# TensorE's products that nobody reads left out of the heads and tails of all stages other than the attentions

## The chip, the cores and the metric

The kernel runs on one core of a Trainium2 chip. The metric is the device time of one launch in microseconds (us). TensorE (PE in the profile) multiplies matrices, and its weight loads have rows of their own (PEld); VectorE is DVE, ScalarE is ACT, GpSimd is POOL, and SP issues the transfers. The profile gives TensorE's granted clock as a share of its full speed: 1.00 is 2.4 GHz and 0.50 is 1.2 GHz.

## The reference

The input x is (4, 256, 256), 1024 tokens of 256 channels, and so is a context `ctx`. Four decoder layers follow each other, each with a self-attention, a cross-attention to the context and a feed-forward part, each on a layer-normed x and added to x:

```python
x = x + _L0_attn_ref(_layernorm(x, axis=-1), ...)      # capped scores
x = x + _L0_xattn_ref(_layernorm(x, axis=-1), ctx_2048, ctx_2048)
x = x + _L0_ffn_ref(...)                               # fp4 weights, gelu
x = x + _L1_attn_ref(...)                              # token and channel mixing, no attention
x = x + _L1_xattn_ref(...)
x = x + _L1_ffn_ref(...)                               # eight experts of different widths, top 2
x = x + _L2_attn_ref(...)                              # 32 heads of 8
x = x + _L2_xattn_ref(_layernorm(x, axis=-1), ctx_2048)
x = x + _L2_ffn_ref(...)                               # sixteen experts, top 4, and a shared one
x = x + _L3_attn_ref(...)                              # 16 heads of 16
x = x + _L3_xattn_ref(...)                             # a scan over the tokens
x = x + _L3_ffn_ref(...)                               # ternary weights, silu
```

## The kernel before

X holds x in SBUF as eight tiles of 128 tokens (`TT` = 8), and HT the normed x with channels in the partitions. The kernel is a row of stages; each is a block in which every engine has its own list of instructions, in the order of the code, tied to the others by semaphores. All engines meet at the end of a block, and none begins the next before the last has come there; the view of waits names the line of the block then (`PEq L1054` and the like). The stages, with the time of the first TensorE entry: `project` and `capped_attention` (layer 0), `cross_attention` (from 153 us), `mlp` (214.9), `mixing` (280.1), `cross_attention` (361.7), `experts1` (416.9), `project_paired` (531.7) and `shifted_attention` (563.9) of layer 2, `cross16` (703.3), `experts2` (799.7), `project_paired` (1111.2) and `shifted_attention` (1146.3) of layer 3, `wkv_scan` (1227.9), and `ternary_mlp` (1273.9).

Most stages begin with a layer norm, `norm_steps`: for each pair g of token tiles VectorE takes the moments (`measure`), ScalarE the root (`root`), VectorE scales into H (`apply`, L300), TensorE turns four 128x128 blocks (`turn`, L363), and ScalarE copies them into HT (`copy`, L331, or as the first of three bf16 parts, L333 to L337 with L305 and L309 on VectorE). The stage's own products wait for two pairs of it (`columns`).

Between these steps TensorE's list holds calls of `warm`, n products of the bf16 identity with itself, 512 columns each, into a bank of PSUM that nobody reads:

```python
    def warm(pe, bank, n):
        for _ in range(n):
            pe.matmul(PS[:, bank, :].rearrange("p (a n) -> p a n", a=4), identb[:],
                      identb[:].rearrange("p (a n) -> p a n", a=1).to_broadcast([P, 4, P]), start=True, stop=True)
```

They wait for nothing and nothing waits for them by a semaphore, but TensorE takes them in order with the rest. All of them have line L241. The attentions (`shifted_attention`) have such calls too, at their head, in their first steps and at their tail (20 products at the tail of a cross-attention, 4 at that of a self-attention).

Of the kernel before, what the change touches and what calls it, by code (L numbers as in the profile page):

```python
# [131 lines left out]
def build_decoder(nc, x, ctx, wa, wb, wl, w2f, vec, rowv, const, out):  # L132
# [105 lines left out]
# [5 lines that stand above are left out]
# [797 lines left out]
    def project_paired(w, hd, V, spread, arrived=None, **norm_of):  # L1040
# [8 lines left out]
        with ExitStack() as st:  # L1049
# [4 lines left out]
            with nc.Block() as block:  # L1054
                @block.tensor
                def _(pe):
                    if arrived is not None:
                        pe.wait_ge(*arrived)
                    warm(pe, 3, 8)
                    norm["turn"](pe, 0)  # L1060
                    warm(pe, 3, 4)
                    norm["turn"](pe, 1)
                    warm(pe, 3, 3)
                    for n, (a, _, j, c) in enumerate(work):
# [22 lines left out]
                        last.then_inc(S["v_proj"], 1)  # L1087
                    warm(pe, 6, 18)

# [244 lines left out]
    def mlp(n, up, down, bias, **norm_of):  # L1334
# [3 lines left out]
        with ExitStack() as st:  # L1338
# [7 lines left out]
            with nc.Block() as block:  # L1346
                @block.tensor
                def _(pe):
# [20 lines left out]

                    warm(pe, 3, 8)  # L1370
                    for g in range(TT // 2):
                        norm["turn"](pe, g)
                        warm(pe, 3, 4)
                    for c in range(NCH):
# [59 lines left out]
    def mixing():  # L1434
# [7 lines left out]
        with ExitStack() as st:  # L1442
# [20 lines left out]
            bank_out = lambda g: (0, 1, 3, 6)[g]  # L1463
            bank_cv = lambda g: (2, 5, 4, 7)[g]

            with nc.Block() as block:
# [101 lines left out]
                def _(pe):  # L1568
# [97 lines left out]
                    for f in range(sum(FB1)):  # L1666
                        if f % 4 == 0:
                            warm(pe, bank_out(1), 1)
                        last = pe.matmul(PS[:, bank_out(0), 0:1], wB("w2")[:, f * P:(f + 1) * P], gelu_b1[:, f:f + 1],
                                         start=f == 0, stop=f == sum(FB1) - 1)  # L1670
                    last.then_inc(S["bias_sum"], 1)
                    warm(pe, bank_out(1), 16)

# [72 lines left out]
    def experts1():  # L1746
# [9 lines left out]
        with ExitStack() as st:  # L1756
# [17 lines left out]
            with nc.Block() as block:  # L1774
# [10 lines left out]
                def _(pe):  # L1785
# [22 lines left out]

                    warm(pe, 0, 8)
                    for c in range(NCH):  # L1810
                        norm["turn"](pe, 2 * c)
                        warm(pe, 0, 4)
                        norm["turn"](pe, 2 * c + 1)
                        warm(pe, 0, 3)
                        norm["columns"](pe, 2 * c + 1)
                        for k in range(KD):
                            last = pe.matmul(PS[:, 2 + c, :], wB("down", KD)[:, k, :], HT[:, k, c * CH:(c + 1) * CH],
                                             start=k == 0, stop=k == KD - 1)
                        last.then_inc(S["narrow"], 1)
# [10 lines left out]

                    warm(pe, 4, 6)
                    pe.wait_ge(S["gates"], d["gates"] + 1)
# [114 lines left out]
    def experts2(sums, over_partitions, scales, replace):  # L1947
# [7 lines left out]
        with ExitStack() as st:  # L1955
# [15 lines left out]
            with nc.Block() as block:  # L1971
# [27 lines left out]
                def _(pe):  # L1999
# [19 lines left out]

                    warm(pe, 7, 8)  # L2020
                    norm["turn"](pe, 0)
                    warm(pe, 7, 4)
                    norm["turn"](pe, 1)
                    warm(pe, 7, 3)
                    norm["columns"](pe, 1)
# [348 lines left out]
    def ternary_mlp(exact, SC, parts):  # L2374
# [5 lines left out]
        with ExitStack() as st:  # L2380
# [6 lines left out]
            with nc.Block() as block:  # L2387
                @block.tensor
                def _(pe):
# [22 lines left out]

                    warm(pe, 3, 8)
                    for g in range(TT // 2):
                        norm["turn"](pe, g)
                        warm(pe, 3, 4)
                    warm(pe, 3, 6)
                    for c in range(NCH):
# [205 lines left out]
```

## Time and profile before

| what | value |
|---|---|
| time, median of 3 runs | 1354.63 us (1352.7 to 1359.07) |
| the profiled execution, its own time | 1354.48 us |
| its span, first to last instruction | 1352.7 us |
| TensorE busy | 1227.5 us, 91% |
| VectorE, ScalarE, GpSimd busy | 57%, 41%, 25% |
| DMA | 47.24 MB, mean 35 GB/s |

The profile comes from one execution. A busy TensorE includes the products that nobody reads, and says nothing of the clock; the row of granted clock does. In a timeline row the first number is the start, the second the length, and what stands in brackets is the idle time before it and who ended it. A float32 product is recorded as two entries (a turn's blocks as one each), so that "x4" of 128x512 in float32 is two products of the program.

### The profile page before, as it was taken

What the parts mean: (1) busy time and instruction counts of PE and PEld (TensorE: products, weight loads), DVE (VectorE), ACT (ScalarE), POOL (GpSimd) and SP (SyncE); (2) the same over time, 40 slices, a digit from 0 to 9 for tenths busy, and PEclk for the clock granted to TensorE, in tenths of its full rate; (3) what the DMA queues carried; (4) which work ended last, traced back from release to release, by engine and by line L of the source; (5) the groups of instructions that cost most, each with busy time, mean ns of one, the idle gap of its engine ahead of it and who ended that gap; (6) DMA issues with size and microseconds to landing.
All of it is one profiled execution on the core that took longest, in us unless ns stands there. A gap on an engine that the chain in (4) does not pass through costs nothing. (4 is left out here: it accounts for less than half of the span.)

```text
span 1352.7 us, 23648 instructions
## 1 busy us (share of the span) xinstructions
PE 1227.5 (91%) x9359; PEld 739.4 (55%) x9374; DVE 769.2 (57%) x2069; ACT 554.3 (41%) x1096; POOL 334.2 (25%) x376
## 2 busy tenths in 40 slices
PE   5878897969998998999998999999999999996898
PEld 3456543658654444566664545555555555663455
DVE  6733586585785346678866745242111126778955
ACT  4777054643354243644444544111111115446453
POOL 2454012000022000445541312232222223451100
PEclk9988998979999999999999998999999999997899
DMA  9000000000220300000000000223322300000000
GB/s 373 0 2 1 1 2 1 0 1 0 117 88 1 125 0 1 1 3 2 3 2 1 2 1 12 68 66 96 95 82 85 106 17 1 2 2 0 0 1 31
DMA packets 13341, 47.24 MB, mean 35 GB/s; under 512 B 1688, under 2 KB 4888, under 8 KB 12464
## 3 DMA queue, kind: packets, MB, share of 16 engines
q1 hardware_dynamic: 13232, 45.74, 10.0%
q8 instruction: 74, 1.21, 0.4%
q14 instruction: 35, 0.29, 0.1%
HBM read 44.59 MB, written 1.15 MB: 34 GB/s over the span
## 5 line engine op out<-in xcount | busy, mean ns | idle before, releaser
L827 ACT ACTIVATE PT<-PS 128x384 f32<-128x384 f32 (+1 forms) x320 | 153.2, 531 | 185.7 <-PE PS L640 138.3
L2007 PE MATMUL PS<-HT,WA 128*128 128x512 f32 x448 | 201.6, 593 | 2.4 <-DVE MO L2085 2.0
L2085 DVE TENSOR_TENSOR MO<-PS,AO 128x512 f32<-128x512 f32 x56 | 38.7, 691 | 205.9 <-ACT AO L2075 205.8
L2075 ACT ACTIVATE AO<-PS 128x512 f32<-128x512 f32 x56 | 33.3, 597 | 247.9 <-PE PS L2007 247.8
L2007 PEld LDWEIGHTS PS<-HT,WA 128*128 128x128 f32 x448 | 84.6, 190 | 87.7 <-issue 82.9
L760 DVE CUSTOM_DVE_ANT_0 junk<-PS,TRI 128x128 bf16<-128x128 f32 (+1 forms) x384 | 112.6, 353 | 4.0 <-PE PS L621 0.2
L241 PE MATMUL PS<-identb 128*128 128x512 bf16 x420 | 105.2, 390 | 4.9 <-PEq L593 1.8
L2015 PE MATMUL PS<-WA,HO 128*128 128x256 f32 x448 | 105.5, 378 | 0.0
L2015 PEld LDWEIGHTS PS<-WA,HO 128*128 128x128 f32 x448 | 84.5, 189 | 34.7 <-issue 24.9
L2140 POOL TENSOR_TENSOR HO<-MO,GR 128x512 f32<-128x512 f32 x44 | 57.8, 1314 | 168.6 <-PE PS L2015 168.6
L621 PE MATMUL PS<-KS,QM 32*128 32x128 f32 (+1 forms) x768 | 86.7, 347 | 7.5 <-DVE QM L794 6.6
L640 PE MATMUL PS<-QM,KS 32*128 32x256 f32 (+1 forms) x768 | 88.5, 347 | 0.0
L799 DVE RECIPROCAL OD<-OD 128x256 f32<-128x256 f32 x40 | 69.9, 1747 | 31.0 <-ACT OD L835 25.9
L868 POOL TENSOR_SCALAR_AFFINE_SELECT PT<-PT 128x512 f32<-128x512 f32 x96 | 60.8, 634 | 99.1 <-ACT PT L827 99.1
L878 POOL TENSOR_TENSOR OD<-OD 128x256 f32<-128x256 f32 x24 | 17.4, 726 | 270.9 <-DVE OD L799 270.9
L621 PEld LDWEIGHTS PS<-KS,QM 32*128 32x128 f32 x768 | 65.8, 184 | 30.2 <-DVE QM L794 16.6
L709 PE MATMUL PS<-PT,CST 128*32 128x256 f32 (+1 forms) x1280 | 75.3, 353 | 0.0
L241 PEld LDWEIGHTS PS<-identb 128*128 128x128 bf16 x420 | 39.2, 100 | 54.4 <-issue 19.4
L640 PEld LDWEIGHTS PS<-QM,KS 32*128 32x128 f32 x768 | 65.6, 184 | 1.9 <-issue 1.2
L709 PE MATMUL PS<-PT,VM 128*32 128x256 f32 (+1 forms) x1024 | 58.3, 345 | 2.0 <-POOL PT L868 1.8
L1115 POOL TENSOR_TENSOR ROT<-RC,RS 128x512 f32<-128x512 f32 x16 | 20.3, 1270 | 149.0 <-DVE RS L1104 147.7
L1931 DVE SCALAR_TENSOR_TENSOR HB<-HA,ROW,GB 128x512 f32<-128x512 f32 x40 | 30.1, 751 | 40.6 <-ACT HA L1866 36.1
(323 smaller groups left out, 2398.1 us busy)
## 6 DMA issues: line engine op xcount, KB each, us to landing
WA<-w2f_in SPq DMA_DIRECT2D x28, 384.0 KB, 4.3
WA<-wl_in SPq DMA_DIRECT2D x1, 5137.0 KB, 15.3
GR<-gate_rows SPq DMA_DIRECT2D x20, 256.0 KB, 3.8
GB<-gate_rows SPq DMA_DIRECT2D x8, 512.0 KB, 7.0
WB<-wb_in SPq DMA_DIRECT2D x1, 3208.0 KB, 19.2
WA<-wa_in SPq DMA_DIRECT2D x1, 2560.0 KB, 14.7
WA<-wa_in SPq DMA_DIRECT2D x1, 1792.0 KB, 15.5
GR<-gate_rows SPq DMA_DIRECT2D x4, 448.0 KB, 3.9
```

Of the source, the lines that this page charges most:

```text
L241: pe.matmul(PS[:, bank, :].rearrange("p (a n) -> p a n", a=4), identb[:], identb[:].rearrange("p (a n) -> p a n", a=1).to_broadcast([P, 4, ...
L621: return pe.matmul(PS[:, s, m * T:m * T + n], queries(U, v)[rows, m * P:(m + 1) * P], keys(U, v)[rows, 0:n], start=True, stop=True, skip_g ...
L640: last = pe.matmul(bank, keys(U, v)[rows, n * P:(n + 1) * P], queries(U, v)[rows, lo:hi], start=n == 0, stop=r > 1, skip_group_check=True, ...
L709: last = pe.matmul(PS[at:at + 32, 7, what * T + lo:what * T + hi], lhs, src, start=what == 0 and v == 0 and n == 0, stop=v == r - 1 and n ...
L760: last = dve.tensor_tensor_reduce(junk[:, s, m * P:m * T + P], PS[:, s, m * T:m * T + (m + 1) * P], TRI[:, (1 - m) * P:T], 1.0, NEG, ALU.a ...
L799: dve.reciprocal(o, o).then_inc(S["at_inv"], 1)
L827: act.activation(PT[:, g % 3, st_slot(k), 0:W], PS[:, st_bank(g, k), 0:W], ACT.Exp, scale=scale).then_inc(S["at_exp"], 1)
L868: pool.affine_select(v, v, [[0, 4], [1, P]], ALU.is_ge, 0.0, base=0, channel_multiplier=-1).then_inc(S["at_masked"], 1)
L2007: last = pe.matmul(PS[:, 2 * c + half, :], chunk(i, half)[:, k * P:(k + 1) * P], HT[:, k, c * CH:(c + 1) * CH], start=k == 0, stop=k == KD ...
L2015: last = pe.matmul(PS[:, 4 + t // 2, (t % 2) * D:(t % 2 + 1) * D], HO[:, c, j * P:(j + 1) * P], chunk(i, 2), start=i == 0 and t % 2 == 0, ...
L2085: dve.tensor_tensor(MO[:, c], PS[:, 2 * c + 1, :], AO[:, c], ALU.mult).then_inc(S["mult_out"], 1)
L2140: pool.tensor_tensor(HO[:, c], MO[:, c], gate[:, c * CH:(c + 1) * CH], ALU.mult).then_inc(S["pool_mark"], 1)
```

## The change

Each `warm` call outside `shifted_attention` goes. 184 of 420 such products go: 24 in `mlp` (8 at the head, 4 behind each turn), 21 in `mixing` (five singles among the twenty products with one column, L1669, and 16 at the tail), 28 in `experts1` (22 at the head, 6 ahead of the turns of the gates), 15 at the head and 18 at the tail of each of the two `project_paired`, 15 at the head of `experts2`, 30 at the head of `ternary_mlp`. Nothing else differs, so that the other engines have the lists that they had.

```diff
--- before.py
+++ after.py
@@ -1056,11 +1056,8 @@
                 def _(pe):
                     if arrived is not None:
                         pe.wait_ge(*arrived)
-                    warm(pe, 3, 8)
                     norm["turn"](pe, 0)
-                    warm(pe, 3, 4)
                     norm["turn"](pe, 1)
-                    warm(pe, 3, 3)
                     for n, (a, _, j, c) in enumerate(work):
 
                         if n == 0:
@@ -1085,7 +1082,6 @@
                             last = pe.matmul(PS[:, 4 + t % 2, 0:D], HT[:, k, t * P:(t + 1) * P], w["v"][:, k, :],
                                              start=k == 0, stop=k == KD - 1)
                         last.then_inc(S["v_proj"], 1)
-                    warm(pe, 6, 18)
 
                 @block.vector
                 def _(dve):
@@ -1367,10 +1363,8 @@
                                                  skip_group_check=True)
                         last.then_inc(S["down_ps"], 1)
 
-                    warm(pe, 3, 8)
                     for g in range(TT // 2):
                         norm["turn"](pe, g)
-                        warm(pe, 3, 4)
                     for c in range(NCH):
                         go_up(0, c)
                     for i in range(n):
@@ -1664,12 +1658,9 @@
                     pe.wait_ge(S["mx_gate"], 2)
                     pe.wait_ge(S["bias_gelu"], 1)
                     for f in range(sum(FB1)):
-                        if f % 4 == 0:
-                            warm(pe, bank_out(1), 1)
                         last = pe.matmul(PS[:, bank_out(0), 0:1], wB("w2")[:, f * P:(f + 1) * P], gelu_b1[:, f:f + 1],
                                          start=f == 0, stop=f == sum(FB1) - 1)
                     last.then_inc(S["bias_sum"], 1)
-                    warm(pe, bank_out(1), 16)
 
                 @block.scalar
                 def _(act):
@@ -1806,12 +1797,9 @@
                                                  wB("core", KD)[:, k, :], start=k == 0, stop=k == KD - 1)
                         last.then_inc(S["o_proj"], 1)
 
-                    warm(pe, 0, 8)
                     for c in range(NCH):
                         norm["turn"](pe, 2 * c)
-                        warm(pe, 0, 4)
                         norm["turn"](pe, 2 * c + 1)
-                        warm(pe, 0, 3)
                         norm["columns"](pe, 2 * c + 1)
                         for k in range(KD):
                             last = pe.matmul(PS[:, 2 + c, :], wB("down", KD)[:, k, :], HT[:, k, c * CH:(c + 1) * CH],
@@ -1828,7 +1816,6 @@
                     for g in range(TT // 2):
                         core(g)
 
-                    warm(pe, 4, 6)
                     pe.wait_ge(S["gates"], d["gates"] + 1)
                     for t in range(TT):
                         last = pe.transpose(PS[0:E, 4 + t // 4, (t % 4) * P:(t % 4 + 1) * P], G[:, t, :], ident)
@@ -2017,11 +2004,8 @@
                                              skip_group_check=True)
                         last.then_inc(S["down_ps"], 1)
 
-                    warm(pe, 7, 8)
                     norm["turn"](pe, 0)
-                    warm(pe, 7, 4)
                     norm["turn"](pe, 1)
-                    warm(pe, 7, 3)
                     norm["columns"](pe, 1)
                     go_up(0, 0)
                     norm["turn"](pe, 2)
@@ -2410,11 +2394,8 @@
                                                  skip_group_check=True)
                         last.then_inc(S["down_ps"], 1)
 
-                    warm(pe, 3, 8)
                     for g in range(TT // 2):
                         norm["turn"](pe, g)
-                        warm(pe, 3, 4)
-                    warm(pe, 3, 6)
                     for c in range(NCH):
                         go_up(0, c)
                     for i in range(n):
```

The head of layer 2's `project_paired` on TensorE, before (L363 is a turn, L1077 the query and key projection, L1085 the value projection):

```order
L1055 UNCONDITIONAL_BRANCH
L241 MATMUL PS<-identb 128x512 x8
L363 MATMUL PS<-CST,H 128x128 x4
L241 MATMUL PS<-identb 128x512 x4
L363 MATMUL PS<-CST,H 128x128 x4
L241 MATMUL PS<-identb 128x512 x3
L1077 MATMUL PS<-HT,WA 128x512 x2
L1085 MATMUL PS<-WA,HT 128x256 x2
```

and after the change, whose line numbers are smaller by three from there on:

```order
L1055 UNCONDITIONAL_BRANCH
L363 MATMUL PS<-CST,H 128x128 x8
L1074 MATMUL PS<-HT,WA 128x512 x2
L1082 MATMUL PS<-WA,HT 128x256 x2
L363 MATMUL PS<-CST,H 128x128 x4
```

The first two turns stand next to each other and are the only work ahead of the projections.

The tail of the same stage and the head of its attention on TensorE, before (L621 is a product of scores):

```order
L1077 MATMUL PS<-HT,WA 128x512 x2
L1085 MATMUL PS<-WA,HT 128x256 x2
L241 MATMUL PS<-identb 128x512 x18
L1054 UNCONDITIONAL_BRANCH
L599 UNCONDITIONAL_BRANCH
L621 MATMUL PS<-KS,QM 128x256 x2
L621 MATMUL PS<-KS,QM 128x128 x2
L621 MATMUL PS<-KS,QM 128x256 x2
L621 MATMUL PS<-KS,QM 128x128 x2
L241 MATMUL PS<-identb 128x512 x8
```

and after the change:

```order
L1074 MATMUL PS<-HT,WA 128x512 x2
L1082 MATMUL PS<-WA,HT 128x256 x2
L1054 UNCONDITIONAL_BRANCH
L599 UNCONDITIONAL_BRANCH
L621 MATMUL PS<-KS,QM 128x256 x2
L621 MATMUL PS<-KS,QM 128x128 x2
L621 MATMUL PS<-KS,QM 128x256 x2
L621 MATMUL PS<-KS,QM 128x128 x2
L241 MATMUL PS<-identb 128x512 x8
```

Eighteen products go from the end of the block; the attention's own eight stay.

The head of `experts1` on TensorE up to the turns of the gates, before (L1817 narrows to 128 channels, L1822 is the router, L1793 an expert's first product, L1805 the core product, L1834 the turns of the gates):

```order
L363 MATMUL PS<-CST,H 128x128 x4
L241 MATMUL PS<-identb 128x512 x3
L1817 MATMUL PS<-HT,WB 128x512 x2
L363 MATMUL PS<-CST,H 128x128 x4
L241 MATMUL PS<-identb 128x512 x4
L363 MATMUL PS<-CST,H 128x128 x4
L241 MATMUL PS<-identb 128x512 x3
L1817 MATMUL PS<-HT,WB 128x512 x2
L1822 MATMUL PS<-WB,HT 128x8 x16
L1793 MATMUL PS<-GH,WB 128x512 x2
L1805 MATMUL PS<-WB,H 128x256 x16
L241 MATMUL PS<-identb 128x512 x6
```

and after the change:

```order
L363 MATMUL PS<-CST,H 128x128 x8
L1805 MATMUL PS<-HT,WB 128x512 x2
L363 MATMUL PS<-CST,H 128x128 x8
L1805 MATMUL PS<-HT,WB 128x512 x2
L1810 MATMUL PS<-WB,HT 128x8 x16
L1784 MATMUL PS<-GH,WB 128x512 x2
L1796 MATMUL PS<-WB,H 128x256 x16
L1821 MATMUL PS<-CST,G 8x128 x8
```

The last two turns follow each other, and the turns of the gates follow the core product directly.

## Rows read from the trace of the kernel before

**Rows 1.** The page: its first line, and TensorE's granted clock in 40 slices.

```profile
span 1352.7 us, 23648 instructions
PEclk9988998979999999999999998999999999997899
```

**Rows 2.** The view of the cores: span and mean granted clock.

```profile
core 0: 1352.7 us, clock 0.963
```

**Rows 3.** The page's groups: the products that nobody reads (busy us, mean ns).

```profile
L241 PE MATMUL PS<-identb 128*128 128x512 bf16 x420 | 105.2, 390 | 4.9 <-PEq L593 1.8
```

**Rows 4.** Windows, TensorE alone: us, busy (entries), granted clock, DMA share, GB/s.

```profile
223.90:229.10 5.20, 0.05 (x1) 0.73 0.00 0
229.10:233.10 4.00, 3.94 (x10) 0.50 0.00 0
...
432.90:436.20 3.30, 0.00 (x0) 0.74 0.00 0
436.20:441.30 5.10, 5.05 (x8) 0.50 0.00 0
...
1257.10:1260.50 3.40, 3.40 (x5) 0.50 0.00 0
```

**Rows 5.** Timeline, TensorE, the start of `mlp`'s products.

```profile
229.16 5.79 PE L1356 MATMUL PS<-parts,WA 128*128 128x512 bf16 x17 [5.22 <-DVE parts L309]
```

**Rows 6.** Windows of all engines (PE, PEld, DVE, ACT, POOL; then clock, DMA).

```profile
361.70:366.70 5.00, 5.00 (x38) 2.64 (x38) 3.67 (x9) 1.25 (x1) 0.00 (x0) 1.00 0.99 365
...
531.70:537.80 6.10, 4.72 (x24) 2.16 (x24) 5.99 (x26) 3.39 (x7) 0.00 (x0) 1.00 0.01 1
537.80:544.00 6.20, 6.20 (x25) 3.98 (x26) 3.82 (x10) 0.60 (x1) 1.26 (x1) 1.00 0.00 0
...
563.90:568.80 4.90, 4.82 (x38) 2.76 (x38) 3.52 (x20) 1.28 (x1) 4.89 (x4) 1.00 0.02 5
...
1111.20:1120.20 9.00, 4.72 (x24) 2.15 (x24) 8.75 (x30) 3.38 (x7) 0.00 (x0) 1.00 0.01 2
```

**Rows 7.** Timeline, the head of layer 2's `project_paired`.

```profile
531.70 1.89 PE L241 MATMUL PS<-identb 128*128 128x512 bf16 x8 [0.78 <-PEq L1774]
...
536.10 0.66 PE L363 MATMUL PS<-CST,H 128*128 128x128 f32 x4 [0.18 <-DVE H L300]
...
537.79 1.98 PE L1077 MATMUL PS<-HT,WA 128*128 128x512 f32 x4 [0.39 <-ACT HT L331]
```

**Rows 8.** Timeline, the same kinds of work elsewhere, at other clocks.

```profile
8.90 1.09 PE L363 MATMUL PS<-CST,H 128*128 128x128 f32 x4 [8.90 <-DVE H L300]
...
436.25 3.78 PE L1793 MATMUL PS<-GH,WB 128*128 128x512 f32 x4 [3.38 <-ACT GH L1856]
...
1273.93 3.36 PE L241 MATMUL PS<-identb 128*128 128x512 bf16 x8 [0.93 <-PEq L2166]
```

**Rows 9.** Timeline, the tail of layer 2's `project_paired` and its attention's start.

```profile
559.41 4.05 PE L241 MATMUL PS<-identb 128*128 128x512 bf16 x18
...
562.10 1.52 ACT L1138 ACTIVATE KS<-ROT,CST 128x512 f32<-128x512 f32 x2 [0.51 <-POOL ROT L1115]
...
563.93 0.95 PE L621 MATMUL PS<-KS,QM 32*128 32x256 f32 x16 [0.47 <-PEq L1054]
```

**Rows 10.** Timeline, the first steps of that attention.

```profile
567.50 1.04 PE L241 MATMUL PS<-identb 128*128 128x512 bf16 x4
567.53 0.08 DVE L760 DVE_READ_ACCUMULATOR2_ANT MX<- 128x1 f32 x1
```

**Rows 11.** Timeline, `experts1`: its head, its core product's end, its first gated product.

```profile
423.07 0.73 DVE L300 TENSOR_SCALAR H<-X,mom,rstd 128x256 f32<-128x256 f32 x2
...
425.26 1.03 PE L241 MATMUL PS<-identb 128*128 128x512 bf16 x4
...
447.48 1.46 PE L241 MATMUL PS<-identb 128*128 128x512 bf16 x6
...
456.84 0.75 DVE L1931 SCALAR_TENSOR_TENSOR HB<-HA,ROW,GB 128x512 f32<-128x512 f32 x1 [4.51 <-DMA GB<-gate_rows]
```

## The prediction

> **What bounds the kernel now.** I read the page first. TensorE is busy for most of the span, and its granted clock is high but not full: the row of tenths holds 9 with an 8 or a 7 here and there [rows 1], and the mean over the span is 0.963 [rows 2]. With only two levels, 2.4 GHz at 1.00 and 1.2 GHz at 0.50, that is 2 x (1 - 0.963) x 1352.7 = 100 us at the lower one. So two things can move the time: what TensorE has to do, and at which of the two clocks it does it. The change touches both. It removes work: 184 of the 420 products that nobody reads, 0.39 us each on average with overlap counted [rows 3]; back to back one takes less, (4.05 - 0.38) / 17 = 0.216 us in the run of 18 at the tail of layer 2's projections [rows 9], with 0.38 for the last one's own length. All 184 come to 39.7 us of TensorE's list. The question is how much of that list something waits for, and what the clock does without it.
>
> I then read windows of TensorE for what a pause does to the clock. In `mlp`, between the head and the first product, TensorE does 0.05 us in 5.2 and the mean clock of that stretch is 0.73, so it fell inside; the next 4.0 us, busy for 3.94, run at 0.50. In `experts1` a pause of 3.3 us gives 0.74, and the next 5.1 us run at 0.50 though TensorE is busy for 5.05. In the scan 3.4 busy us run at 0.50 [rows 4]. So the clock comes back only some time after the work does, and that time is paid by whoever waits for TensorE.
>
> Then the stretches that the change empties, in the windows of all engines. All heads have the clock at 1.00 now: 531.7 to 537.8 with 4.72 us of TensorE in 6.1, and the work behind it, 537.8 to 544.0, busy for 6.20 of 6.20 at 1.00. So have the starts of the attentions at 361.7 and 563.9 [rows 6]. Those following stretches are the ones to watch: TensorE has no idle time in them, so it bounds them, and a slower clock is paid in full.
>
> **The change part by part.**
>
> *What the removed products hold up.* In most heads nothing. The turn at 536.10 is released by H from VectorE after 0.18 us of idle time, and the projection at 537.79 by ScalarE's copy after 0.39 us [rows 7]: TensorE had done its idle products before either. The same pattern stands at the heads of `mlp`, `experts2` and the other `project_paired`. At the tails nothing either: the 18 products end at 559.41 + 4.05 = 563.46, but ScalarE's last copy of keys ends at 562.10 + 1.52 = 563.62, and the next block begins 0.3 us after that [rows 9]. Without them the block ends when it did. The tail of `mixing` and that of layer 3 look alike. Two places are left, both in `experts1`. H of the last pair is complete at 423.07 + 0.73 = 423.80, but four idle products begin at 425.26 and only then comes the last turn [rows 11]: 4 x 0.216 = 0.86 us gained. And six products stand between the core product and the turns of the gates [rows 11]; from there the way goes over the gates' trip through memory to the first gated product, which waits 4.51 us for that transfer [rows 11], so their 6 x 0.216 = 1.30 us are on the path. Gains: 2.2 us.
>
> *Where the clock falls.* In the head at 531.7, 15 of the removed products make 1.89 + 1.03 + 0.81 = 3.73 of the 4.72 busy us (a run of four lasts 3 x 0.216 + 0.38, a run of three 2 x 0.216 + 0.38). What stays is 0.99 us of turns in 6.1 [rows 6, 7]; the nearest rows are the two pauses of 5.2 and 3.3 us in which the clock fell [rows 4], so I take it as fallen. The other heads are built alike (`experts1`, `experts2`, layer 3, `ternary_mlp`). At the two tails of the projections 4.05 us of products become a pause that lasts until 563.93, 4.4 us [rows 9]; in `mixing` the 21 products leave only products with one column ahead of the attention. Eight places in all: five heads, three tails. The ninth, `mlp`, is free: its first product waits 5.22 us for VectorE's third part [rows 5] and begins at the lower clock already [rows 4], as it will.
>
> *What a restart costs.* After a pause like ours the work ran at 0.50 for 4.0 and for 5.1 us [rows 4]; I take 4.5. Half of the work of that time is left over at its end: 2.25 us. Bounds: 3.4 us [rows 4] give 1.7, 5.1 give 2.55. That TensorE does need twice as long shows in the same shape at both clocks: four entries of 128x512 in 1.98 us [rows 7] and in 3.78 [rows 8], eight idle products in 1.89 [rows 7] and in 3.36 [rows 8].
>
> *Whether it is hidden.* Behind the five heads TensorE is busy without a break, as at 537.8 to 544.0 [rows 6], and ScalarE's chain of the projections waits for it (turns 2 and 3 come after the first projections in its list). In the attentions the idle products that stay, 8 and then 4 and 4, are in TensorE's list between the scores: at 567.50 four of them run until 568.54, while VectorE's last maximum, for which the next turn waits, is done at 567.53 + 0.08 = 567.61 [rows 10]. So TensorE is the later one there too, by 0.9 us, and at half clock by more. I hide nothing.
>
> *The turns.* At the heads the second turn itself runs at half clock, and the first product waits for it: 1.09 us against 0.66 [rows 8, 7], 0.43 for each of the five.
>
> *The sum.* Heads 5 x (2.25 + 0.43) = 13.4; tails 3 x 2.25 = 6.75; gains -2.2. Together +18.0 us. Against the profiled execution's own 1354.48 that is 1372.5; it lies 0.15 under the median of the runs shown, which changes nothing.
>
> *A rule against this sum.* The mean clock over the span is 0.963 [rows 2], so the lower level already costs up to 50 us, half of the 100. The Trainium skill, page "TensorE: Matmul & The Clock Gate", section "Part 1: The HAM clock gate", says that for modelling, the penalty of the clock's ramp stays under 1% of a typical kernel's span. The trace of before does not agree with it as a rule for such a kernel of many stages: 50 us are 3.7%. By the page the sum would be an estimate of less than 13.5 us more and the time under 1368.1.
>
> **The rivals.**
>
> *Cheaper restarts at the attentions (chance 0.2).* The three tails leave shorter pauses (4.4 us) with full work on both sides, and VectorE and GpSimd are busy at the attentions' starts: 3.52 and 4.89 of 4.9 us [rows 6]. If the clock holds there, or VectorE's maxima and GpSimd's staging take as long anyway, the three tails cost nothing: 18.0 - 6.75 = 11.3, 1365.7. Against it: the 3.3 us pause that was enough [rows 4]. The Trainium skill's bound above, 1368.1, lies near this case.
>
> *Longer restarts (0.13).* The attentions' products are narrow (32 rows) and broken by waits, so the clock may need twice as long there; and in the two expert stages the router's narrow products come soon after the head. With one more 3.4 us of half clock at three of the eight, and at the attentions' starts 0.9 us more of waiting: 18.0 + 3 x 1.7 + 2 x 0.9 = 24.9, 1379.4.
>
> *Not slower (0.05).* The clock does not fall where the products go, because the neighbours' work and the turns suffice. For it: from 1111.2 to 1120.2 TensorE is idle for almost half of the time, busy for 4.72 of 9.0 us, and the clock stays 1.00 [rows 6]. Then only the gains are left, 1354.5 - 2.2 = 1352.3. It decides at the granted clock of the first six us behind each head: 1.00 there makes this one right. Against it: there the idle time lay in pieces between products that now go, and only 0.99 of 6.1 is left.
>
> *Faster (0.02).* The tails hold up the ends of their blocks after all, since the meeting of the engines takes TensorE's drain in: 18 + 18 + 16 products, 11.2 us, and with the clock unharmed 1352.3 - 11.2 = 1341.1. ScalarE's end at 563.62, after the products' [rows 9], speaks against all of it.
>
> **How the numbers follow.** The forecast, eight restarts of 1.7 to 2.55 us in full, has 0.60 and by itself reaches from 18.0 - 8 x 0.55 = 13.6 to 18.0 + 8 x 0.3 = 20.4 more, so 1368 to 1375; with the cheap case below it and most of the dear one above I give 1362 to 1380. What a measurement of this kernel can tell from no change is 0.5%, 6.8 us. Slower by more: the forecast, the dear case, and nearly all of the cheap one, 0.91. Within: the case of an unharmed clock and the end of the cheap one, 0.07. Faster: 0.02.
>
> **What the profile after would show.** The granted clock at 0.50 for 3.4 to 5.1 us at the start of the projections of layers 2 and 3, of `experts1`, `experts2` and `ternary_mlp`, and of the attentions behind the two projections and behind `mixing`; a mean clock near 0.94: eight times 4.5 us and some 20 us of pauses on top of the 100 give 156 us, 1 - 156 / (2 x 1370.7) = 0.943. The first four entries of the projections take near 3.7 us instead of 1.98. The ends of the blocks with a tail are set by ScalarE or VectorE as before. `mlp`'s products begin as long after their block's start as now. I am wrong if the clock stays 1.00 behind the heads, if the attentions' first exponentials come no later than now (then their restarts are hidden), or if TensorE shows idle time for other engines behind the heads.

## The result and the profile after

The changed kernel takes 1372.48 us (median of 4 runs, 1369.29 to 1374.09) against 1356.76 us of the kernel before, timed beside it (4 runs, 1352.7 to 1359.07). The ratio is 1.0116, with a 95% interval of 1.0082 to 1.015: slower by 15.7 us. The runs of the kernel before fall into two groups with nothing between them: of its 23 runs on the chip of the later experiments six took 1353.2 to 1354.3 us and seventeen 1357.2 to 1360.5, and of the four here two lie in each. So a median moves by a few us with the mix. Lowest against lowest the change costs 16.6 us here (1369.29 - 1352.70) and 15.9 on the other chip (1369.10 - 1353.20). The profiled execution took 1372.37 us, 17.89 more than that of before, which belongs to the lower group. The page of the kernel after, its first line, the busy times, TensorE's clock, and the group of products that nobody reads:

```profile
span 1370.6 us, 23281 instructions
PE 1209.5 (88%) x9175; PEld 732.6 (53%) x9190; DVE 768.5 (56%) x2069; ACT 554.8 (40%) x1096; POOL 334.7 (24%) x376
PEclk9888998989898998999999999999999998997799
...
L241 PE MATMUL PS<-identb 128*128 128x512 bf16 x236 | 60.7, 401 | 1.7 <-PEq L412 1.1
```

The view of its cores:

```profile
core 0: 1370.6 us, clock 0.938
```

The products that nobody reads are called idle products from here on. They take 44.5 us less of TensorE's time (105.2 [rows 3] to 60.7), but its busy time falls by only 18.0 (1227.5 to 1209.5): all other work takes 26.5 us longer. The clock says why: 0.963 [rows 2] has become 0.938, so 2 x 0.062 x 1370.6 = 170 us lie at the lower level, where it was 100. Half of these 70 us would be 35, twice what the profiled executions differ by: a part of them lies in pauses, in which the clock costs nothing.

Windows of TensorE alone in the kernel after (stretch, length, busy time with entries, granted clock, DMA share, GB/s). In this order: the start of layer 1's cross-attention, in two parts; the first products of `experts1`; the head of layer 2's `project_paired` and what follows it; its attention; the head of `experts2` and what follows; what follows the head of layer 3's `project_paired`; its attention; the first products of `ternary_mlp`:

```profile
366.60:372.20 5.60, 5.60 (x26) 0.50 0.94 345
372.20:377.00 4.80, 4.42 (x31) 1.00 0.97 420
...
430.60:433.60 3.00, 2.95 (x4) 0.50 0.00 0
...
538.10:544.20 6.10, 2.20 (x8) 0.61 0.00 1
544.20:549.70 5.50, 5.40 (x9) 0.50 0.00 0
...
573.00:577.00 4.00, 3.93 (x23) 0.57 0.01 2
...
809.00:815.20 6.20, 1.77 (x8) 0.78 0.00 1
815.20:819.30 4.10, 4.08 (x5) 0.50 0.00 0
...
1131.60:1136.80 5.20, 5.17 (x8) 0.50 0.00 0
...
1160.20:1164.10 3.90, 3.82 (x22) 0.56 0.00 0
...
1300.20:1304.00 3.80, 3.50 (x9) 0.50 0.00 0
```

The same work in the kernel before, for `experts2` and `ternary_mlp` (layer 1's cross-attention and layer 2's two places are in [rows 6]; `experts1` and layer 3's two places show 1.00 over 3.0, 5.2 and 3.9 us as well):

```profile
805.80:809.90 4.10, 4.10 (x14) 1.00 0.00 0
...
1284.30:1288.10 3.80, 3.76 (x18) 1.00 0.02 4
```

Where before showed 1.00 with TensorE full, the first 3.0 to 5.6 us behind each head and tail are now at 0.50 (0.57 over 4.0 us at the attention is 3.4 us of it). The timeline of the same head in layer 2, TensorE (start, length, and in brackets the idle time before it):

```profile
540.89 1.09 PE L363 MATMUL PS<-CST,H 128*128 128x128 f32 x4 [3.57 <-DVE H L300]
542.50 1.11 PE L363 MATMUL PS<-CST,H 128*128 128x128 f32 x4 [0.52 <-DVE H L300]
544.30 3.78 PE L1074 MATMUL PS<-HT,WA 128*128 128x512 f32 x4 [0.69 <-ACT HT L331]
...
550.06 1.88 PE L1074 MATMUL PS<-HT,WA 128*128 128x512 f32 x4
```

The four entries that took 1.98 us [rows 7] take 3.78. The same four at 550.06 are back at 1.88.

**The loss stage by stage.** ScalarE loads a table of functions near the start of each stage, which gives a mark that both traces have. ScalarE's timeline at that mark in layer 2's `project_paired`, kernel before:

```profile
531.66 1.28 ACT L326 ACT_TABLE_LOAD   x1 [7.81 <-PEq L1774]
```

and kernel after:

```profile
538.06 1.28 ACT L326 ACT_TABLE_LOAD   x1 [7.80 <-PEq L1765]
573.03 1.28 ACT L827 ACT_TABLE_LOAD   x1 [0.27 <-PEq L1054]
```

At the first the kernel after is 6.40 us late. In the table each number is the time from one mark to the next, less the same in the trace of before; all runs of this study are in it. The mark of `cross16` lies 16 us inside it, that of layer 0's cross-attention 10.

| stage | after | after again | heads out | tails out | 8 columns | path out | first 8 out | fill | none |
|---|---|---|---|---|---|---|---|---|---|
| to layer 0's cross-attention | 5.86 | 4.08 | 0.00 | 2.66 | 0.21 | -0.12 | 5.02 | -0.43 | 0.86 |
| layer 0 cross-attention | 0.00 | 0.00 | 0.01 | 0.01 | 0.02 | 0.02 | 0.01 | 0.01 | 3.44 |
| `mlp` | 0.04 | -0.02 | -0.02 | 0.13 | 0.00 | -0.03 | 0.02 | -0.86 | -0.19 |
| `mixing` | -1.01 | 0.00 | 0.01 | -0.96 | 0.02 | 0.00 | 0.23 | 0.63 | -0.10 |
| layer 1 cross-attention | 2.64 | 2.15 | 0.00 | 2.64 | 2.15 | 0.01 | -0.01 | 0.00 | 5.18 |
| `experts1` | -1.13 | -1.15 | -0.33 | -0.70 | 0.85 | -3.06 | 0.47 | -3.62 | -1.13 |
| layer 2 `project_paired` | 2.74 | 2.47 | 3.12 | -0.01 | 3.15 | -0.01 | -0.01 | 0.00 | 2.59 |
| layer 2 attention | 1.60 | 1.61 | -0.03 | 2.92 | 1.66 | -0.02 | -0.04 | -0.04 | 2.56 |
| `cross16` | -1.42 | 0.16 | 0.22 | -1.42 | -1.42 | -1.41 | -1.42 | 0.21 | 1.19 |
| `experts2` | 2.12 | 2.89 | 2.32 | 0.00 | 2.32 | 0.01 | -0.01 | -0.02 | 1.98 |
| layer 3 `project_paired` | 2.51 | 2.89 | 2.61 | -0.02 | 2.61 | -0.01 | 0.58 | 0.00 | 2.45 |
| layer 3 attention | 1.62 | 1.62 | -0.01 | 2.84 | 1.62 | -0.02 | -0.02 | -0.01 | 2.82 |
| `wkv_scan` | 0.00 | -0.01 | 0.01 | 0.01 | 0.01 | 0.01 | 0.00 | 0.00 | -0.72 |
| `ternary_mlp` | 2.32 | 2.53 | 3.18 | 0.00 | 2.36 | 0.01 | 1.32 | 0.00 | 2.06 |
| sum | 17.90 | 19.21 | 11.09 | 8.10 | 15.56 | -4.63 | 6.13 | -4.14 | 22.98 |

The first line and that of `cross16` hold stages whose code nobody touched except in the last column, and yet they differ, the first by up to 5.9 us (5.86 in one execution of the changed kernel, 0.00 with the heads out), the other between -1.42 and 0.22. That part of a difference of two profiled executions is no effect of an edit: the lower clock takes other pieces of them from one execution to the next. `mixing` shows it too: -1.01 in the first execution of the changed kernel and 0.00 in the second. Its tail is not where that comes from: the last stretch of the stage, from ScalarE's last mark in it to the attention's, took 14.80 us before and 14.81 after. So only the lines of changed stages are read for the mechanism, and the timed ratio for the size.

### The profile page after: what moved, and what is told of

Its sections match the earlier page's. It is cut to its first block and busy times, and to the rows that moved or that the text cites. A ratio compares the mean times of both kernels' runs of the same rounds, so it can differ in the third digit from the quotient of the medians.

```text
span 1370.6 us, 23281 instructions
## 1 busy us (share of the span) xinstructions
PE 1209.5 (88%) x9175; PEld 732.6 (53%) x9190; DVE 768.5 (56%) x2069; ACT 554.8 (40%) x1096; POOL 334.7 (24%) x376
## 3 DMA queue, kind: packets, MB, share of 16 engines
HBM read 44.59 MB, written 1.15 MB: 33 GB/s over the span
## 5 line engine op out<-in xcount | busy, mean ns | idle before, releaser
L621 PE MATMUL PS<-KS,QM 32*128 32x128 f32 (+1 forms) x768 | 87.5, 351 | 15.3 <-PEq L1054 8.7
L621 PEld LDWEIGHTS PS<-KS,QM 32*128 32x128 f32 x768 | 66.2, 186 | 37.9 <-issue 19.9
L878 POOL TENSOR_TENSOR OD<-OD 128x256 f32<-128x256 f32 x24 | 17.5, 727 | 272.5 <-DVE OD L799 272.5
L363 PE MATMUL PS<-CST,H 128*128 128x128 f32 x128 | 29.4, 377 | 45.4 <-DVE H L300 45.4
L241 PE MATMUL PS<-identb 128*128 128x512 bf16 x236 | 60.7, 401 | 1.7 <-PEq L412 1.1
```

What stands on the lines that cost most here:

```text
L621: return pe.matmul(PS[:, s, m * T:m * T + n], queries(U, v)[rows, m * P:(m + 1) * P], keys(U, v)[rows, 0:n], start=True, stop=True, skip_g ...
```

## The experiments

The times are medians. The ratios compare all runs with those of the kernel before on the same chip (median 1358.17 us of 17 runs for the first four experiments, 1358.45 of 23 for the others). They lie within 0.0003 of the ratios of the means and up to 0.0011 above those of the medians, because of the two groups; a difference in us given with a ratio is that ratio's share of the median of before. Diffs are against the kernel before.

### Heads only, tails only

Heads: the idle products of all heads go, and the six ahead of the gates' turns; the tails stay.

```diff
-                    warm(pe, 3, 8)
                     norm["turn"](pe, 0)
-                    warm(pe, 3, 4)
                     norm["turn"](pe, 1)
-                    warm(pe, 3, 3)
...
-                    warm(pe, 4, 6)
```

> Only the products at the five stage heads, at the head of mlp and ahead of the turns of the gates go; the three tails stay. Theory (the clock falls and its return is paid in full behind each head, a slow turn costs 0.1 us, not 0.43): heads 5 x (2.25 + 0.11) = 11.8, less 2.2 gained in experts1, +9.6 us against the kernel before. Rival (the loss sits at the attentions, whose work is narrow): heads cost little, +2 us or less.

Measured: 1366.41 us, ratio 1.0067 (1.0044 to 1.0091), +9.1 us for the 9.6 expected, clock 0.947. The windows at layer 2's head, in the kernel with the heads out:

```profile
531.40:537.50 6.10, 2.20 (x8) 0.67 0.01 1
537.50:542.90 5.40, 5.33 (x9) 0.50 0.00 0
```

Tails: only these go.

```diff
-                    warm(pe, 6, 18)
...
-                        if f % 4 == 0:
-                            warm(pe, bank_out(1), 1)
...
-                    warm(pe, bank_out(1), 16)
```

> Only the tails of mixing and of the two project_paired go (with the five singles in mixing). Theory: the clock is at 0.50 for 3.4 to 5.6 us at the start of three attentions, 2.6 + 1.7 + 1.7 = +6.0 us. Rival (VectorE's maxima and GpSimd's staging hide it): 0. Rival (the tails hold the ends of their blocks): faster than before, by up to 11.

Measured: 1364.84 us, ratio 1.0048 (1.0029 to 1.0067), +6.5 us for the 6.0 expected. The window at the start of layer 2's attention, in the kernel with the tails out:

```profile
567.70:573.70 6.00, 5.99 (x28) 0.50 0.01 4
```

The two parts add up, 1.0067 x 1.0048 = 1.0115 against the 1.0116 of the whole. Each interval reaches 2.6 to 3.3 us to either side, so this does not show that the restarts are independent of each other, and the stages show that they are not quite so (below). In the column of the tails both `project_paired` stand at -0.01 and -0.02: their blocks end when they did, and the whole loss (2.64, 2.92, 2.84) is in the attentions behind. The rivals that put nothing there, or a gain, fall. The attentions of layers 2 and 3 lose more with the heads kept (2.92 and 2.84) than with the heads gone too (1.60 and 1.62), and the windows show why: the clock stays at 0.50 for 6.0 us there, and for 3.4 in the changed kernel, with the same instructions in the attention. `ternary_mlp` loses 3.18 with only the heads out, 2.32 and 2.53 in the changed kernel. How long the clock takes to return is not the same at each restart; what sets it stays open.

### The same products, eight columns wide

All 184 stay in the lists, in their order, but stream 8 columns of the identity instead of 512.

```diff
+    def narrow(pe, bank, n):
+        for _ in range(n):
+            pe.matmul(PS[:, bank, 0:8], identb[:], identb[:, 0:8], start=True, stop=True)
...
-                    warm(pe, 3, 8)
+                    narrow(pe, 3, 8)
                     norm["turn"](pe, 0)
-                    warm(pe, 3, 4)
+                    narrow(pe, 3, 4)
```

> All 184 products stay in the list, but stream 8 columns instead of 512. Theory (it is the streaming that keeps the clock up): the clock falls at all eight places as in the changed kernel, mean clock 0.94, +14 to +17 us against the kernel before. Rival (any product in the list keeps TensorE from a costly wake after a wait, whatever it streams): as the kernel before, within 3 us, mean clock 0.96.

Measured: 1371.25 us, ratio 1.0105 (1.0085 to 1.0125), +14.3 us, clock 0.941: as without them, and as expected. TensorE's timeline at layer 2's head with eight columns (line numbers are five higher here):

```profile
534.95 0.34 PE L246 MATMUL PS<-identb 128*128 128x8 bf16 x8 [0.78 <-PEq L1779]
...
541.14 3.78 PE L1082 MATMUL PS<-HT,WA 128*128 128x512 f32 x4 [0.63 <-ACT HT L336]
```

Eight of them take 0.34 us where the wide ones took 1.89 [rows 7], and the projection behind takes the same 3.78 us as with none. What held the clock was TensorE's streaming, not the presence of instructions in its list.

### Only the products on the path of `experts1`

Ten products go: the four ahead of the last turn and the six ahead of the gates' turns.

```diff
                         norm["turn"](pe, 2 * c)
-                        warm(pe, 0, 4)
+                        if c == 0:
+                            warm(pe, 0, 4)
...
-                    warm(pe, 4, 6)
```

> Only ten products of experts1 go: the four ahead of its last turn and the six ahead of the turns of the gates; all others stay. Theory: they are on the path and the neighbours keep the clock at 1.00, so 0.86 + 1.30 = 2.2 us faster than before; the turns of the gates begin 1.3 us sooner behind the core product. Rival (the clock falls here as well): slower by 0 to 1.

Measured: 1354.36 us (12 runs), ratio 0.9972 (0.9958 to 0.9985), -3.8 us (-5.7 to -2.0) for the -2.2 expected; the stage is 3.06 us shorter. TensorE's timeline in `experts1` with these ten out:

```profile
422.88 1.98 PE L1818 MATMUL PS<-HT,WB 128*128 128x512 f32 x4 [0.39 <-ACT HT L331]
...
426.47 1.98 PE L1818 MATMUL PS<-HT,WB 128*128 128x512 f32 x4
428.29 4.45 PE L1823 MATMUL PS<-WB,HT 128*128 128x8 f32 x32
436.11 3.78 PE L1793 MATMUL PS<-GH,WB 128*128 128x512 f32 x4 [3.37 <-ACT GH L1856]
...
456.15 1.12 PE L1799 MATMUL PS<-HB,WB 128*128 128x512 f32 x2 [2.39 <-DVE HB L1931]
```

and the same rows of the kernel before:

```profile
423.00 1.98 PE L1817 MATMUL PS<-HT,WB 128*128 128x512 f32 x4 [0.39 <-ACT HT L331]
...
427.41 1.98 PE L1817 MATMUL PS<-HT,WB 128*128 128x512 f32 x4
429.24 3.63 PE L1822 MATMUL PS<-WB,HT 128*128 128x8 f32 x32
...
457.65 1.38 PE L1799 MATMUL PS<-HB,WB 128*128 128x512 f32 x2 [2.44 <-DVE HB L1931]
```

The four give 4.41 - 3.59 = 0.82 us between the two narrow products, as the forecast's 0.86. But the router's 32 products behind them, which need 3.63 us before, need 4.45 now, because the lower clock comes earlier relative to them; the first expert's product stands at 436.11 against 436.25, and the stage itself began 0.13 us earlier, which leaves nothing of it. The six come through: the first gated product starts at 456.15 instead of 457.65, which from the stage's mark (416.75 and 416.88) is 39.40 instead of 40.77, 1.37 us earlier. The other 1.7 us of the stage's 3.06 are found behind it, in the windows. Kernel before:

```profile
458.00:462.00 4.00, 4.00 (x6) 0.57 1.01 389
```

and with the ten out:

```profile
458.00:462.00 4.00, 4.00 (x11) 1.00 1.03 408
```

Before, TensorE waited 2.44 us for the gates' transfer and then ran at half clock; with the ten out it waited 2.39 us and did not. Nor does it in the changed kernel, at 1.00 there in both executions. But with the heads out, where `experts1` has the same code as in the changed kernel, TensorE does run at half clock there, as this window of that kernel shows:

```profile
457.00:461.00 4.00, 3.67 (x6) 0.67 0.92 370
```

So the 1.7 us come and go from one execution to the next, and I count them to neither side. Over the ten profiled executions of this study the clock fell there in all three that still have the six (before, tails out, first 8 out), in that with eight columns and in that with the heads out; it held in the other five, all without the six. Whether leaving them out makes the fall rarer stays open. What is shown is the ratio and the 1.37 us.

### The changed kernel again

The whole change as in the diff ahead of the prediction, run on another chip.

> The changed kernel again, beside the kernel before on one chip. Heads alone gave 1.0067 and tails alone 1.0048; if the two parts are independent, the whole is 1.0115 (+15.6 us). Rival (they share restarts, since a tail's clock and the next head's are the same fall): clearly less, 1.009 or under.

Measured: 1372.58 us, ratio 1.0111 (1.0091 to 1.0131), +15.1 us, clock 0.937, beside the 1.0115 expected; the rival's 1.009 or under is just outside the interval. The changed stages sum to 15.0 us in its column (2.15 - 1.15 + 2.47 + 1.61 + 2.89 + 2.89 + 1.62 + 2.53), which is what was timed; in the first execution they give 14.4.

### Only the first eight of each head

The five calls of eight products go; those between the turns and behind them stay. The expectation speaks of five heads and 40 products, but `project_paired` is used twice and the call in `mlp` goes too, so that it is six heads and 48 products: 372 of the 420 are left in the page of this run.

```diff
-                    warm(pe, 3, 8)
                     norm["turn"](pe, 0)
                     warm(pe, 3, 4)
```

> Of each head only the first eight products go (five heads, 40 products); the runs of four and three behind the turns stay, and tails too. Theory: the pause ahead of the first turn is 3 to 4 us, the length of those that lowered the clock, so the clock falls at some heads, but the products behind the turns run while it is low and take part of the time to its return: less than the heads' 9.1 us, +2 to +6. Rival (only the last products ahead of the real work matter): within 1 us of the kernel before.

Measured: 1361.04 us (12 runs), ratio 1.0022 (1.0003 to 1.0041), +3.0 us, inside the 2 to 6 expected. The window at layer 2's head without the first eight:

```profile
536.70:543.00 6.30, 2.67 (x15) 1.00 0.02 4
```

With seven wide products between the turns the clock stays at 1.00 here, where with the eight entries of the turns alone it fell. In the column only `ternary_mlp` (1.32), layer 3's head (0.58) and `experts1` (0.47) lose; there the clock did fall, and the products behind the turns ran while it was low (four of them in 1.91 us at layer 3's head, where four take 1.03 at full clock). All losses together, 2.4 us, are about a fifth of what the heads cost in their five stages when all of it goes (10.9): the products between the turns and behind them hold most of the clock. The ratio's 3.0 us fit that. Whether the first eight alone would do as well was not run.

### Ten out, and idle products put where the clock fell before

On top of the ten: 22 more in `mlp` behind its last turn, in the pause of 5.2 us [rows 4, 5], and 14 in `experts1` behind the router, in the pause of 3.3 us [rows 4].

```diff
                         warm(pe, 3, 4)
+                    warm(pe, 3, 22)
...
                         last.then_inc(S["route_logits"], 1)
+                    warm(pe, 0, 14)
```

> The ten products on the path in experts1 go, and 36 new ones stand where the kernel before lets the clock fall: 22 behind the last turn of mlp, in its 5.2 us pause, and 14 between the router and the first expert's product, in the pause of 3.3 us. Theory: mlp's first products run at 1.00, 2.0 us won; experts1's 5.1 us of half clock go, up to 2.5 us; with the 3.8 us that leaving out the ten gave, 5.8 to 8.3 us faster than before, 0.9940 to 0.9957. Rival (the falls have another cause than the pause, the router's narrow products for one, or the new products are on the path): no better than leaving out the ten, 0.9972.

Measured: 1354.25 us (12 runs), ratio 0.9969 (0.9954 to 0.9983): the same as without the 36, and a miss. TensorE's timeline in `mlp` with the fill:

```profile
228.59 1.24 PE L1356 MATMUL PS<-parts,WA 128*128 128x512 bf16 x5 [0.30 <-DVE parts L309]
230.35 2.76 PE L1356 MATMUL PS<-parts,WA 128*128 128x512 bf16 x12 [0.52 <-DVE parts L309]
234.40 1.48 PE L1365 MATMUL PS<-WA,AP 128*128 128x256 bf16 x12 [1.29 <-DVE AP L1391]
```

and in `experts1`:

```profile
427.77 4.24 PE L1824 MATMUL PS<-WB,HT 128*128 128x8 f32 x32
431.86 5.92 PE L241 MATMUL PS<-identb 128*128 128x512 bf16 x14
437.62 1.88 PE L1794 MATMUL PS<-GH,WB 128*128 128x512 f32 x4
```

In `mlp` the clock held: 17 entries in 4.0 busy us instead of 5.79 [rows 5]. But the next product then waited 1.29 us for VectorE, and the stage won 0.86 us for the 2.0 expected (`mixing` behind it took 0.63 longer, which is within what that stage varies by). In `experts1` the clock had already fallen under the router's products, which keep TensorE busy but stream eight columns each (128x8); the 14 ran at half clock, 5.92 us instead of 14 x 0.216 = 3.0, and held up the first expert's product, which from the stage's mark started 2.0 us later than in the kernel with only the ten out (437.62 - 416.22 against 436.11 - 416.75). By then the clock was back, and its four entries took 1.88 us instead of 3.78, so that the fill neither won nor lost much.

### None of the 420

`warm` issues nothing, in the attentions too.

```diff
-        for _ in range(n):
+        for _ in range(0):
```

> All 420 such products go, the attentions' 236 too. Theory: besides the whole change's +15.6 us the attentions lose their start, but no longer carry 8, 4, 4 and 4 products between the first scores, which are on the path at 1.9 and 1.04 us each: five attentions, clock restarts longer (+1 us each), products gone (-2 to -4 us each); about the changed kernel's time, within 8 us. Rival (the attentions' own products pay for themselves): slower than the changed kernel by over 5 us.

Measured: 1377.7 us, ratio 1.0153 (1.013 to 1.0175), +20.8 us, mean clock 0.905. The median is 5.1 us over that of the changed kernel's repeat, which is within the 8 us of the theory and over the 5 of the rival: as they were put, the two overlap. The attentions' own products do pay for themselves, by little. Its window at the start of layer 1's cross-attention:

```profile
365.80:371.00 5.20, 3.85 (x24) 0.50 1.01 367
```

It stands at 0.50 in this stretch and in the two of 5 us behind it, where the changed kernel, with the attentions' own idle products, had it at 1.00 after 5.6. The 236 products inside the attentions are worth less each than the 184 outside: 5.1 / 236 = 0.02 us against 15.1 / 184 = 0.08.

## Why the prediction was right

**The mechanism held at each of its eight places.** The clock stood at 0.50 behind the five heads and three tails that the windows above show, for 3.0 to 5.6 us (forecast 3.4 to 5.1), and the stages lost about half of that; the mean clock was 0.938 for 0.943. The cost of each is close to half of its stretch, plus the turn: layer 2's projections 5.4 / 2 = 2.7 with 2.74 measured for the stage, layer 3's 5.2 / 2 = 2.6 with 2.51, `experts2` 4.1 / 2 = 2.05 with 2.12, layer 1's attention 5.6 / 2 = 2.8 with 2.64, and at the attentions of layers 2 and 3 0.57 and 0.56 over 4.0 and 3.9 us mean 3.4 us at the lower level: 1.7 with 1.60 and 1.62. In `experts1` the head cost 3.06 - 1.13 = 1.9 beside the kernel with only the ten out. At `ternary_mlp` 3.8 / 2 = 1.9 and the slower turns (0.59, below) stand against 2.32. Restarts and turns were put at 18.0 + 2.15 = 20.15 us; by stages they are 17.5 in the first execution (15.55 in seven stages and 1.9).

**What it said would cost nothing cost nothing.** `mlp` began at the lower clock as it does now, and is within 0.04 us. The tails held up no block: 571.25 + 1.52 = 572.77 for ScalarE's last copy, and 573.03 for the next block's first instruction, 0.26 us behind it. ScalarE's row in the kernel after:

```profile
571.25 1.52 ACT L1134 ACTIVATE KS<-ROT,CST 128x512 f32<-128x512 f32 x2 [0.51 <-POOL ROT L1111]
```

**The term that was too large: the slow turn, 0.43 at each of five heads.** The turn did take 1.11 us instead of 0.66. But from the second turn's start to the first projection it is 544.30 - 542.50 = 1.80 us after and 537.79 - 536.10 = 1.69 before [rows 7]: 0.11. From the stage's mark to the first projection it is 6.24 against 6.13, so the 0.11 is all that the two turns cost. The same distance grew by 0.11 in `experts1` and 0.12 in `experts2`, and not at all in layer 3 (9.02 for 9.03). ScalarE's timeline shows where the rest went; kernel before:

```profile
536.95 0.30 ACT L326 ACTIVATE std<-mom,CST 128x2 f32<-128x2 f32 x1 [0.92 <-DVE mom L293]
537.15 0.58 ACT L331 ACTIVATE HT<-PS 128x512 f32<-128x512 f32 x1
```

and kernel after:

```profile
543.35 0.29 ACT L326 ACTIVATE std<-mom,CST 128x2 f32<-128x2 f32 x1 [0.74 <-DVE mom L293]
543.65 0.60 ACT L331 ACTIVATE HT<-PS 128x512 f32<-128x512 f32 x1
```

Before, the turn was over at 536.10 + 0.66 = 536.76, but ScalarE had the root of the next pair ahead of the copy in its list and copied at 537.15, 0.39 us later. After, the turn is over at 542.50 + 1.11 = 543.61 and the copy begins at 543.65. The slack of 0.39 us took in most of the slower turn. The prediction's step "the first product waits for it" read the turn's rows and not ScalarE's. Only `ternary_mlp`, whose products wait for more turns, lost more. TensorE's row of its first product, kernel before (its mark at 1273.90):

```profile
1284.34 1.03 PE L2398 MATMUL PS<-parts,WA 128*128 128x512 bf16 x4
```

and kernel after (its mark at 1289.48):

```profile
1300.51 1.06 PE L2382 MATMUL PS<-parts,WA 128*128 128x512 bf16 x2 [2.34 <-DVE parts L309]
```

That is 10.44 and 11.03 us, 0.59 more. All five together, the forecast's 2.15 becomes 0.9.

**A reading that was wrong.** "All heads have the clock at 1.00 now" does not hold for `ternary_mlp`: its first eight idle products took 3.36 us [rows 8], twice the 1.89 of the same eight in layer 2 [rows 7]. There the idle products did not keep the clock up but brought it back before the first real product, which ran at 1.00 as the window above shows. The restart that the forecast put there came all the same.

**The gains of 2.2 us.** With the ten out the stage won 3.06, but not as forecast: of 0.86 and 1.30 the second came through (1.37), the first was found (0.82) and lost again in the router, and 1.7 came from a stretch that stayed at full clock.

**The sum and the time.** 18.0 us were forecast; 15.7 and 15.1 were timed. The sum was 2.3 to 2.9 us too large. By the stages of the first execution (14.4) the turns were put 1.2 too high and the restarts 1.5 (16.5 for 18.0, mostly the attentions of layers 2 and 3 with 1.60 and 1.62 for 2.25 each), and the gains 0.9 too low. The time itself was hit within 0.1 us by luck: the base, 1354.48, is an execution of the lower group and lies 2 to 4 us under the medians of the kernel before (1356.76, 1358.17, 1358.45), and the two errors cancel.

**The rivals.** The cheaper restarts at the attentions fall: the tails alone cost 6.5 us, against 6.75 forecast. The unharmed clock falls at its own point of decision, the granted clock behind the heads. The tails as a brake on their blocks fall. Longer restarts did not make the sum: in the changed kernel's first execution the stretches at 0.50 lasted at most 5.6 us, and the costs that lay above the forecast's bound of 2.55 were 2.64 and 2.74. They do exist: 2.89 at two places in the repeat, 2.92 at layer 2's attention (6.0 us at 0.50) with only the tails out, 3.12 at layer 2's head with only the heads out, and over 15 us at 0.50 without the attentions' own idle products. The Trainium skill, page "TensorE: Matmul & The Clock Gate", section "Part 1: The HAM clock gate", has the ramp under 1% of a typical kernel's span, which made an estimate of less than 13.5 us for the change; the timed 15.1 and 15.7 us lie over it, and the 170 us at the lower level cost up to 85, 6.2% of the span. The same section says that how many matmuls run at the lower clock when a kernel starts varies from run to run. The traces here show such a variation in the middle of the kernel: untouched stages differ by up to 5.9 us.

## What to carry to other kernels

A product that nobody reads was free here where TensorE would wait anyway, and there it was worth 0.08 us on average; on the path it costs its 0.216 us, so the two kinds are told apart one by one: the best version here keeps 410 and drops 10 (36 more changed nothing that the runs can tell). A restart cost about half of the half-clock stretch that follows if TensorE bounded what came next, and little or nothing was won by preventing it where TensorE then waited for another engine. Two profiled executions are compared stage by stage, and the untouched stages are looked at first, as they show what a difference between two executions is worth.

## What the runs showed of the hardware that was not expected

- Products of eight columns did nothing for the clock: 1.0105 with all 184 of them, 1.0116 and 1.0111 with none.
- TensorE can be busy without a break and still fall to the lower clock: it did so under the router's 32 products of eight columns, which took 3.63 us before, 4.45 with the ten out and 4.24 with the fill. Windows inside them, kernel with the ten out:

```profile
429.30:430.30 1.00, 1.00 (x11) 1.00 0.00 0
...
431.30:432.30 1.00, 1.00 (x6) 0.50 0.00 0
```

- At layer 2's head seven wide products and the turns (2.67 busy us of 6.3) went with a clock of 1.00; the turns alone went with a fall. Their 2.20 busy us of 6.1 are no measure of the difference, since the turns ran at the lower clock by then (1.09 and 1.11 us for 0.66).
- The same instructions behind the same pause ran at 0.50 for 3.4 us in one kernel and for 6.0 in another (layer 2's attention, changed kernel and tails out).
- Stages whose code is the same took up to 5.9 us more or less from one execution to the next, by where in them the clock fell (mean clock between 80 and 90 us 0.68 before and 0.60 after).
